# The weights of the second projection pass are loaded into another buffer, without a gate

## The chip, the cores and the metric

One Trainium2 chip, all 8 cores of it, which run the same program on different data. The metric is the device time in microseconds (us) of the slowest core.

## What is computed

One transformer layer over x of 4 x 4096 x 1024: self-attention with 16 heads, a residual and a layer norm, then a mixture of 16 experts (6 of them chosen per token), a residual and a layer norm. Cut to what matters:

```python
# L0_attn_x: (4, 4096, 1024); Wq, Wk, Wv: (1024, 1024); expert_w: (16, 1024, 1024)
q = (x @ Wq.T).reshape(N, S, H, hd).transpose(0, 2, 1, 3)
k = (x @ Wk.T).reshape(N, S, H, hd).transpose(0, 2, 1, 3)
v = (x @ Wv.T).reshape(N, S, H, hd).transpose(0, 2, 1, 3)
attn = softmax(einsum('nhqd,nhkd->nhqk', q, k) / sqrt(hd), axis=3)
x = _layernorm(x + einsum('nhql,nhld->nhqd', attn, v).transpose(0, 2, 1, 3).reshape(N, S, D))
...
for e in range(E):
    out = out + x @ expert_w[e] * gate[:, e:e + 1]
```

## The kernel before

Each core takes one of the four sequences and one half of its queries: it computes K and V for all 4096 tokens of the sequence and Q for its own 2048. There are three stages, and TensorE goes through them in program order:

1. Projections, in `proj_pass`, called for K, then V, then Q. Each pass loads one weight matrix of 1024 x 1024 (L186) and then goes through sections of 512 tokens: 8 sections for K and V, 4 for Q. A section is one load of activations (x, 1024 KB as bfloat16, L200), cast from float32 on its way, into one of two halves of a staging buffer (`xstage`). Then follow 8 groups of 8 matmuls of 128x512 (L220 for K and Q, L241 for V), each group into one of four PSUM banks, and one VectorE copy a group (L256).
2. Attention: 2 halves of the queries x 8 pairs of heads x 32 blocks of keys. TensorE computes scores (L290), ScalarE the exponentials (L350, L353), TensorE the weighted sums and the denominators (L310, L322). The operand of the scores is read from `QO`, where Q's pass put it.
3. For each of two blocks of 8 token tiles: layer norm, transposes and routing, and the 16 experts (L639), then the second layer norm.

SBUF is a few large tensors that are used again from stage to stage. `RC` (s_RC in the profile) holds during the projections the two x halves (columns 0 to 8191) and the weights `wT` (columns 8192 to 16383). `QO` (s_QO) has 16384 columns and holds Q, later the attention's output; until Q's pass writes it, nothing is in it. `RA` takes K, `RB` takes V.

The order of the loads is that of GpSimd's queue, which holds all of them: weights of K, 8 sections of x, weights of V, 8 sections of x, weights of Q, 4 sections, then 16 copies that cast the experts' weights in HBM. GpSimd issues them in this order, and one that waits holds up all that stand behind it. `tS` counts TensorE's finished groups, 8 to a section. The load of x waits until all groups but the last 8 that are queued so far are done (`ts_need = max(0, ctS.v - 8)`): section s can be loaded when section s-2 is finished, and it is the same across passes. The load of the weights waits for all groups queued so far, that is for the end of the pass before, since all three passes use `wT`:

```python
wt_gate = ctS.v
```

TensorE waits, ahead of each group, for the weights (gW0) and for its section of x (gX0 or gX1), and for the copy that frees its bank (vE).

Of the kernel before, what the change touches and what calls it, by code (L numbers as in the profile page):

```python
# [18 lines left out]
CH = 8  # L19
# [14 lines left out]
def build():  # L34
# [22 lines left out]
    v_wT = {"K": d_wkT.rearrange("(c p) j -> p c j", c=CH),  # L57
            "V": d_wvT.rearrange("(c p) j -> p c j", c=CH),
            "Q": d_wqT.rearrange("(c p) j -> p c j", c=CH)}
# [4 lines left out]
    def alloc(name, shape, dtype, psum=False):  # L64
        cm = nc.psum_tensor(name, shape, dtype) if psum else nc.sbuf_tensor(name, shape, dtype)
        t = cm.__enter__()
        cms.append(cm)
        return t
# [16 lines left out]
    QO = alloc("s_QO", [128, CH * TOK], dt.bfloat16)  # L85
# [8 lines left out]
    def bank(i, lo=0, hi=512):  # L94
        return PS[:, i * 512 + lo: i * 512 + hi]

    def xstage(par):
        return RC[:, par * 4096:(par + 1) * 4096]

    wT = RC[:, 8192:16384]  # L100
# [52 lines left out]
    cgC, ctS, ctV, csE, cvE = (Ctr() for _ in range(5))  # L153
# [7 lines left out]
    def q(eng, fn):  # L161
        SC[eng].append(fn)
# [15 lines left out]
    q("vector", f)  # L178

    def proj_pass(kind, nsect):  # L180
        wt_gate = ctS.v

        def fw(g, wsrc=v_wT[kind], wt_gate=wt_gate):
            if wt_gate > 0:
                g.wait_ge(tS, wt_gate)
            g.dma_start(out=wT.rearrange("p (c j) -> p c j", c=CH),  # L186
                        in_=wsrc).then_inc(gW[0], 16)
        q("gpsimd", fw)
        cgW[0].v += 16
        w_done = cgW[0].v  # L190
        xsrc = v_xqf if kind == "Q" else v_xfm

        for s in range(nsect):
            par = s % 2
            ts_need = max(0, ctS.v - 8)

            def fx(g, s=s, par=par, ts_need=ts_need, xsrc=xsrc):
                if ts_need > 0:
                    g.wait_ge(tS, ts_need)
                g.dma_start(out=xstage(par).rearrange("p (c t) -> p c t", c=CH),  # L200
                            in_=xsrc[:, :, s * 512:(s + 1) * 512]).then_inc(gX[par], 16)
            q("gpsimd", fx)
            cgX[par].v += 16
            x_done = cgX[par].v

            for u in range(8):
                b = ctS.v % 4
                ve_need = ctS.v - 3

                if kind in ("K", "Q"):  # L210
                    jc = u

                    def ft(t, jc=jc, b=b, par=par, x_done=x_done, w_done=w_done,
                           ve_need=ve_need):
                        t.wait_ge(gW[0], w_done)
                        t.wait_ge(gX[par], x_done)
                        if ve_need > 0:
                            t.wait_ge(vE, ve_need)
                        for dc in range(CH):
                            ins = t.matmul(  # L220
                                bank(b),
                                wT[:, dc * 1024 + jc * 128: dc * 1024 + (jc + 1) * 128],
                                xstage(par)[:, dc * 512:(dc + 1) * 512],
                                start=(dc == 0), stop=(dc == CH - 1))
                        ins.then_inc(tS, 1)
                    if kind == "K":
                        dst = RA[:, jc * SQ + s * 512: jc * SQ + (s + 1) * 512]
                    else:
                        dst = QO[:, jc * TOK + s * 512: jc * TOK + (s + 1) * 512]
                else:  # L230
                    tt, jh = u // 2, u % 2
                    kt = s * 4 + tt

                    def ft(t, tt=tt, jh=jh, b=b, par=par, x_done=x_done,
                           w_done=w_done, ve_need=ve_need):
                        t.wait_ge(gW[0], w_done)
                        t.wait_ge(gX[par], x_done)
                        if ve_need > 0:
                            t.wait_ge(vE, ve_need)
                        for dc in range(CH):  # L240
                            ins = t.matmul(  # L241
                                bank(b),
                                xstage(par)[:, dc * 512 + tt * 128:
                                            dc * 512 + (tt + 1) * 128],
                                wT[:, dc * 1024 + jh * 512: dc * 1024 + (jh + 1) * 512],
                                start=(dc == 0), stop=(dc == CH - 1))
                        ins.then_inc(tS, 1)
                    dst = RB[:, kt * D + jh * 512: kt * D + (jh + 1) * 512]

                q("tensor", ft)  # L250
                ctS.v += 1
                te_after = ctS.v

                def fv(v, dst=dst, b=b, te_after=te_after):
                    v.wait_ge(tS, te_after)
                    v.tensor_copy(dst, bank(b)).then_inc(vE, 1)  # L256
                q("vector", fv)
                cvE.v += 1

    proj_pass("K", SQ // 512)  # L260
    proj_pass("V", SQ // 512)
    proj_pass("Q", TOK // 512)
    p1_ve = cvE.v
    p1_ts = ctS.v
# [7 lines left out]
    for h in range(2):  # L272
        for c in range(NPAIR):
            p = h * NPAIR + c
# [545 lines left out]
```

## Time and profile before

| | us |
|---|---|
| median of 3 runs | 2977.89 |
| all runs | 2975.08, 2977.89, 3146.5 |
| the profiled execution, its own time | 2977.37 |
| its span on the slowest core (core 5) | 2975.8 |
| K pass, TensorE, from the first to the last matmul | 29.7 to 142.7 |
| V pass | 170.1 to 282.8 |
| Q pass | 307.4 to 364.5 |

All times inside the execution are counted from the start of the span. The span is that of the slowest core; its own time lies 1.6 us above. Attention runs to about 1636, the third stage to the end of the span.

### The profile page before, as it was taken

The page shows a single profiled execution, that of the slowest core. Times are in us where ns is not written, and L with a number is a line of the kernel's source. Part 1 is how long each engine was busy: PE and PEld are TensorE (multiplying, and loading weights), DVE is VectorE, ACT ScalarE, POOL GpSimd, SP SyncE. Part 2 cuts the span into 40 slices and gives each one's busy share as a digit, 9 for nine tenths or more (in the row PEclk, how much of TensorE's full clock was granted, in tenths as well). Part 3 has the DMA queues.
Part 4 walks back from the last instruction along what each step waited for, and adds up shares of the span by engine and source line. Part 5 has one row for each costly group of instructions (what it writes and reads, how often), then busy time and mean ns, then how long its engine had stood idle before and what let it go on. Part 6 is the DMA issues. An engine that isn't in the chain of part 4 may idle for free.

```text
span 2975.8 us, 31964 instructions; the slowest of 8 cores (2956.2 to 2975.8 us)
## 1 busy us (share of the span) xinstructions
PE 2366.3 (80%) x12032; PEld 897.2 (30%) x12032; DVE 719.1 (24%) x1555; ACT 1120.3 (38%) x1153; POOL 59.7 (2%) x80
## 2 busy tenths in 40 slices
PE   6978889888888888888888343799996343799996
PEld 2433322222222222222222111344442111344442
DVE  2323200000000000000000434233336434233336
ACT  0000089888888888888888101000000101000000
POOL 1000100000000000000000000000000000000000
PEclk9989899999999999999999666899998666899998
DMA  6464799960000000000000200221223100221221
GB/s 87 62 94 67 100 110 114 110 82 1 1 1 1 1 1 1 1 1 1 1 1 1 92 15 7 85 85 57 85 85 106 43 14 7 85 85 57 85 85 57
DMA packets 48017, 146.90 MB, mean 49 GB/s; under 512 B 2752, under 2 KB 23264, under 8 KB 46848
## 3 DMA queue, kind: packets, MB, share of 16 engines
q0 software_dynamic: 43264, 128.09, 23.4%
q1 hardware_dynamic: 4608, 16.78, 1.6%
q8 instruction: 103, 1.69, 0.2%
q14 instruction: 42, 0.34, 0.0%
HBM read 197.32 MB, written 41.94 MB: 80 GB/s over the span
## 4 chain that ended last, share of the span: by engine, by line
PE 61%; ACT 16%; DVE 9%; issue 9%; DMA 4%; DVEq 1%; ACTq 0%; POOL 0%; SPq 0%; POOLq 0%
PE s_PS L639 30%; PE s_PS L290 11%; ACT s_RC L353 9%; PE s_PS L220 6%; PE s_PS L310 5%; ACT s_RC L350 5%; PE s_PS L322 4%; PE s_PS L241 4%; DMA s_RC<-xfm 2%; DVE s_RC L462 2%; PE s_PS L377 1%; DMA s_RC<-xqf 1%; DMA s_RB<-ewb 1%; DVE s_RA L653 1%; DVE s_RC L469 1%
## 5 line engine op out<-in xcount | busy, mean ns | idle before, releaser
L639 PE MATMUL s_PS<-s_RB,s_QO 128*128 128x512 bf16 x4096 | 933.5, 391 | 138.2 <-DVE s_gates L595 67.4
L290 PE MATMUL s_PS<-s_QO,s_RA 64*128 64x512 bf16 x2048 | 598.4, 397 | 104.7 <-ACT s_RC L353 70.8
L350 ACT ACTIVATE s_RC<-s_PS,s_cb 128x1024 bf16<-128x1024 f32 x512 | 570.6, 1115 | 196.4 <-PE s_PS L290 187.3
L639 PEld LDWEIGHTS s_PS<-s_RB,s_QO 128*128 128x128 bf16 x4096 | 407.7, 100 | 660.1 <-issue 211.6
L353 ACT ACTIVATE s_RC<-s_PS,s_cb 128x1024 bf16<-128x1024 f32 x512 | 567.0, 1107 | 0.2
L310 PE MATMUL s_PS<-s_RC,s_RB 128*64 128x512 bf16 x2048 | 330.2, 401 | 10.7 <-ACT s_RC L353 10.7
L697 ACT ACTIVATE s_tE<-s_tB 128x1 f32<-128x1 f32 x16 | 3.2, 203 | 883.1 <-DVE s_tB L689 883.1
L322 PE MATMUL s_PS<-s_RC,s_ozb 128*64 128x512 bf16 x2048 | 318.0, 389 | 0.0
L367 DVE CAST s_QO<-s_PS 128x1024 bf16<-128x1024 f32 x16 | 19.6, 1225 | 1189.2 <-PE s_PS L322 1189.2
L290 PEld LDWEIGHTS s_PS<-s_QO,s_RA 64*128 64x128 bf16 x2048 | 118.1, 94 | 540.8 <-issue 540.8
L656 DVE SCALAR_TENSOR_TENSOR s_RB<-s_PS,s_gates,s_RA 128x1024 f32<-128x1024 f32 x128 | 164.2, 1283 | 275.3 <-PE s_PS L639 275.3
L220 PE MATMUL s_PS<-s_RC 128*128 128x512 bf16 x768 | 170.0, 385 | 54.3 <-DMA s_RC<-xfm 29.7
L659 DVE SCALAR_TENSOR_TENSOR s_RA<-s_PS,s_gates,s_RB 128x1024 f32<-128x1024 f32 x112 | 143.8, 1284 | 272.4 <-PE s_PS L639 272.4
L516 PE MATMUL s_PS<-s_idb,s_RC 128*128 128x128 bf16 x128 | 16.2, 305 | 190.9 <-ACT s_RC L508 190.9
L322 PEld LDWEIGHTS s_PS<-s_RC,s_ozb 128*64 128x64 bf16 x2048 | 123.1, 113 | 107.2 <-issue 10.8
L310 PEld LDWEIGHTS s_PS<-s_RC,s_RB 128*64 128x64 bf16 x2048 | 75.3, 109 | 239.8 <-issue 239.8
L350 ACT ACT_TABLE_LOAD x1 | 1.3, 1283 | 366.3 <-PE s_PS L290 366.3
L241 PE MATMUL s_PS<-s_RC 128*128 128x512 bf16 x512 | 112.7, 384 | 27.4 <-DMA s_RC<-xfm 27.4
L490 ACT ACTIVATE s_tE<-s_tB 128x1 f32<-128x1 f32 x16 | 3.2, 203 | 348.2 <-DVE s_tB L481 348.2
L220 PEld LDWEIGHTS s_PS<-s_RC 128*128 128x128 bf16 x768 | 75.9, 99 | 147.9 <-issue 60.0
L615 POOL DMA_DIRECT2D s_RB<-ewb x32 | 28.3, 885 | 2516.0 <-PE s_PS L377 1290.9
L241 PEld LDWEIGHTS s_PS<-s_RC 128*128 128x128 bf16 x512 | 50.5, 99 | 89.6 <-issue 30.6
(76 smaller groups left out, 594.2 us busy)
## 6 DMA issues: line engine op xcount, KB each, us to landing
s_RB<-ewb POOLq DMA_DIRECT2D x32, 2048.0 KB, 10.3
ewb<-ew POOLq DMA_DIRECT2D x16, 2048.0 KB, 169.3
s_RC<-xfm POOLq DMA_DIRECT2D x16, 1024.0 KB, 11.4
s_RC<-xtm SPq DMA_DIRECT2D x16, 512.0 KB, 3.6
y<-s_RC SPq DMA_DIRECT2D x16, 512.0 KB, 2.6
s_RC<-xqf POOLq DMA_DIRECT2D x4, 1024.0 KB, 17.7
s_RC<-wkT POOLq DMA_DIRECT2D x1, 2048.0 KB, 18.0
s_RC<-wvT POOLq DMA_DIRECT2D x1, 2048.0 KB, 18.2
```

Of the source, the lines that this page charges most:

```text
L220: ins = t.matmul(bank(b), wT[:, dc * 1024 + jc * 128: dc * 1024 + (jc + 1) * 128], xstage(par)[:, dc * 512:(dc + 1) * 512], start=(dc == 0 ...
L241: ins = t.matmul(bank(b), xstage(par)[:, dc * 512 + tt * 128: dc * 512 + (tt + 1) * 128], wT[:, dc * 1024 + jh * 512: dc * 1024 + (jh + 1) ...
L290: ins = t.matmul(PS[:, head * 1024 + qc * 512: head * 1024 + (qc + 1) * 512], RA[rows, c * SQ + kc * 128: c * SQ + (kc + 1) * 128], QO[row ...
L310: t.matmul(PS[orow, 2048 + qc * 512: 2048 + (qc + 1) * 512], RB[:, kcp * D + hh * 64: kcp * D + (hh + 1) * 64], P[:, head * 1024 + qc * 51 ...
L322: ins = t.matmul(PS[orow, 3072 + qc * 512: 3072 + (qc + 1) * 512], ozb[:, :], P[:, head * 1024 + qc * 512: head * 1024 + (qc + 1) * 512], ...
L350: sc.activation(P[:, 0:1024], PS[:, 0:1024], AF.Exp, bias=cb3[:, :], scale=0.125).then_inc(sE, 1)
L353: sc.activation(P[:, 1024:2048], PS[:, 1024:2048], AF.Exp, bias=cb3[:, :], scale=0.125).then_inc(sE, 1)
L377: ins = t.transpose(PS[:, 3072 + sl * 128: 3072 + (sl + 1) * 128], zs[:, sl * 128:(sl + 1) * 128], idf[:, :])
L462: v.scalar_tensor_tensor(u_f32[:, sg * 64:(sg + 1) * 64], PS[:, pcol + sg * 64: pcol + (sg + 1) * 64], rz[:, t_i * NH + sg: t_i * NH + sg ...
L639: ins = t.matmul(PS[:, pb + jh * 512: pb + (jh + 1) * 512], QO[:, dc * TOK + t_i * 128: dc * TOK + (t_i + 1) * 128], wbuf(par)[:, dc * 102 ...
L656: v.scalar_tensor_tensor(accB(tt), PS[:, pb: pb + 1024], g, accA(tt), ALU.mult, ALU.add).then_inc(vE, 1)
L659: v.scalar_tensor_tensor(accA(tt), PS[:, pb: pb + 1024], g, accB(tt), ALU.mult, ALU.add).then_inc(vE, 1)
```

## The change

V's weights go into the first 8192 columns of `QO` instead of `wT`, and their load waits for nothing. V's matmuls read them from there. The loads of K's and Q's weights are as before: K's waits for nothing, since nothing is queued ahead of it, and Q's waits for the end of V's pass. The loads of x and their waits are as before. V's and Q's x loads keep their places in the queue.

```diff
 def proj_pass(kind, nsect):
-        wt_gate = ctS.v
-
-        def fw(g, wsrc=v_wT[kind], wt_gate=wt_gate):
+        if kind == "V":
+            wtile = QO[:, 0:8192]
+            wt_gate = 0
+        else:
+            wtile = wT
+            wt_gate = ctS.v if kind == "Q" else 0
+
+        def fw(g, wsrc=v_wT[kind], wt_gate=wt_gate, wtile=wtile):
             if wt_gate > 0:
                 g.wait_ge(tS, wt_gate)
-            g.dma_start(out=wT.rearrange("p (c j) -> p c j", c=CH),
+            g.dma_start(out=wtile.rearrange("p (c j) -> p c j", c=CH),
                         in_=wsrc).then_inc(gW[0], 16)
...
-                                wT[:, dc * 1024 + jc * 128: dc * 1024 + (jc + 1) * 128],
+                                wtile[:, dc * 1024 + jc * 128: dc * 1024 + (jc + 1) * 128],
...
-                                wT[:, dc * 1024 + jh * 512: dc * 1024 + (jh + 1) * 512],
+                                wtile[:, dc * 1024 + jh * 512: dc * 1024 + (jh + 1) * 512],
```

GpSimd's queue before, from the weights of K (wkT) to the last loads of the projections (xfm is x for K and V, xqf is x for Q):

```order
L186 DMA s_RC<-wkT 128x8x1024
L200 DMA s_RC<-xfm 128x8x512 x2
L200 DMA s_RC<-xfm 128x8x512 [waits tS] x6
L186 DMA s_RC<-wvT 128x8x1024 [waits tS]
L200 DMA s_RC<-xfm 128x8x512 [waits tS] x8
L186 DMA s_RC<-wqT 128x8x1024 [waits tS]
L200 DMA s_RC<-xqf 128x8x512 [waits tS] x4
```

And now, the same stretch of the same queue:

```order
L191 DMA s_RC<-wkT 128x8x1024
L205 DMA s_RC<-xfm 128x8x512 x2
L205 DMA s_RC<-xfm 128x8x512 [waits tS] x6
L191 DMA s_QO<-wvT 128x8x1024
L205 DMA s_RC<-xfm 128x8x512 [waits tS] x8
L191 DMA s_RC<-wqT 128x8x1024 [waits tS]
L205 DMA s_RC<-xqf 128x8x512 [waits tS] x4
```

No entry has changed its place; the load of wvT has another target and has lost its wait.

TensorE's order before, at the seam from K to V (L220 is K's last group, L241 is V):

```order
L220 MATMUL s_PS<-s_RC 128x512 [waits gW0,gX1,vE]
L220 MATMUL s_PS<-s_RC 128x512 x7
L241 MATMUL s_PS<-s_RC 128x512 [waits gW0,gX0,vE]
L241 MATMUL s_PS<-s_RC 128x512 x7
L241 MATMUL s_PS<-s_RC 128x512 [waits gW0,gX0,vE]
```

And now:

```order
L225 MATMUL s_PS<-s_RC 128x512 [waits gW0,gX1,vE]
L225 MATMUL s_PS<-s_RC 128x512 x7
L246 MATMUL s_PS<-s_QO,s_RC 128x512 [waits gW0,gX0,vE]
L246 MATMUL s_PS<-s_QO,s_RC 128x512 x7
L246 MATMUL s_PS<-s_QO,s_RC 128x512 [waits gW0,gX0,vE]
```

The matmuls and their waits are the same; V's read one operand from s_QO.

## Rows read from the trace of the kernel before

**Rows 1.** The page: its head, and the chain that ended last, by engine.
```profile
span 2975.8 us, 31964 instructions; the slowest of 8 cores (2956.2 to 2975.8 us)
...
PE 61%; ACT 16%; DVE 9%; issue 9%; DMA 4%; DVEq 1%; ACTq 0%; POOL 0%; SPq 0%; POOLq 0%
```

**Rows 2.** TensorE's waits, 0 to 380 us: us in total, times, longest.
```profile
PE s_PS L220 <- DMA s_RC<-xfm: 29.7, 1, 29.7
PE s_PS L241 <- DMA s_RC<-xfm: 27.4, 1, 27.4
PE s_PS L220 <- DMA s_RC<-xqf: 24.6, 1, 24.6
```

**Rows 3.** The chain in order of time, 0 to 600 us: start, us, what.
```profile
29.72 112.93 PE s_PS L220 x512
144.04 25.77 DMA s_RC<-xfm
170.06 112.74 PE s_PS L241 x512
```

**Rows 4.** GpSimd's timeline, 100 to 150 us: start, us, instruction, idle before it.
```profile
101.74 0.87 POOL L200 DMA_DIRECT2D s_RC<-xfm  x1 [12.94 <-PE s_PS L220]
115.55 0.87 POOL L200 DMA_DIRECT2D s_RC<-xfm  x1 [12.94 <-PE s_PS L220]
143.18 0.87 POOL L186 DMA_DIRECT2D s_RC<-wvT  x1 [26.75 <-PE s_PS L220]
```

**Rows 5.** Line L200, the two loads behind the weights of K, of V, of Q.
```profile
DMA to landing us min/median/max: 24.0/27.0/30.1
...
DMA to landing us min/median/max: 25.8/27.9/30.0
...
DMA to landing us min/median/max: 23.0/25.0/27.1
```

**Rows 6.** Line L200, the load of K's last section, issued at 115.55.
```profile
DMA to landing us min/median/max: 11.3/11.3/11.3
```

**Rows 7.** Stretches around the gap ahead of V: busy us by engine, PEclk, DMA share, GB/s.
```profile
142.00:146.00 4.00, 0.64 (x3) 0.10 (x1) 0.69 (x1) 0.00 (x0) 2.62 (x3) 1.00 0.00 0
146.00:148.00 2.00, 0.00 (x0) 0.00 (x0) 0.00 (x0) 0.00 (x0) 0.00 (x0) 0.74 0.82 93
148.00:170.00 22.00, 0.00 (x0) 0.00 (x0) 0.00 (x0) 0.00 (x0) 0.00 (x0) 0.50 1.10 154
170.00:174.00 4.00, 3.94 (x10) 1.49 (x11) 0.27 (x1) 0.00 (x0) 0.00 (x0) 0.50 0.93 154
174.00:176.00 2.00, 2.00 (x11) 0.79 (x10) 0.59 (x2) 0.00 (x0) 0.00 (x0) 0.94 0.03 4
```

**Rows 8.** Line L186, the load of V's weights.
```profile
DMA to landing us min/median/max: 18.2/18.2/18.2
```

**Rows 9.** Stretches with one x load in flight, and with V's first three loads.
```profile
118.00:128.00 10.00, 10.00 (x48) 4.50 (x46) 4.15 (x6) 0.00 (x0) 0.00 (x0) 1.00 0.80 107
146.00:176.00 30.00, 5.94 (x19) 2.28 (x20) 0.86 (x2) 0.00 (x0) 0.00 (x0) 0.54 0.99 140
```

**Rows 10.** Line L200, the load of V's third section, issued at 186.63.
```profile
DMA to landing us min/median/max: 9.7/9.7/9.7
```

**Rows 11.** Groups of the page: count, busy us, mean ns of one, idle before.
```profile
L290 PE MATMUL s_PS<-s_QO,s_RA 64*128 64x512 bf16 x2048 | 598.4, 397 | 104.7 <-ACT s_RC L353 70.8
L241 PE MATMUL s_PS<-s_RC 128*128 128x512 bf16 x512 | 112.7, 384 | 27.4 <-DMA s_RC<-xfm 27.4
```

**Rows 12.** TensorE's waits on core 6, 0 to 380 us.
```profile
PE s_PS L241 <- DMA s_RC<-xfm: 24.3, 1, 24.3
```

**Rows 13.** Stretches of the third stage: the first tiles, and experts of the first block.
```profile
1636.00:1892.00 256.00, 99.83 (x469) 44.57 (x468) 102.46 (x377) 22.89 (x48) 3.58 (x4) 0.66 0.16 50
1892.00:2270.00 378.00, 374.19 (x1726) 169.03 (x1725) 148.77 (x137) 1.22 (x6) 11.48 (x13) 1.00 0.22 76
```

## The prediction

> **What bounds the kernel now.** I read the views from the outside in. The page comes first: a span of 2975.8 us, with the chain that ended last made of TensorE for 61%, ScalarE for 16% and DMA for 4% [rows 1]. That small DMA share is what the change touches, so the next view is TensorE's waits over the three projection passes. It has three long ones, and all three are for a load of activations: 29.7 us ahead of K, 27.4 us ahead of V, 24.6 us ahead of Q [rows 2]. The chain in order of time shows how the middle one is built [rows 3]: TensorE ends K at 29.72 + 112.93 = 142.65, GpSimd then issues V's weights and, behind them at 144.04, the x load of V's section 0, which lands 25.77 us later, at 169.81, and the first V matmul starts at 170.06. From 142.65 to 170.06 is 27.41 us in which VectorE and ScalarE have nothing either. Everything later in the program hangs on TensorE's order, so what this gap loses, the whole span loses.
>
> GpSimd's own rows show why [rows 4]: the loads of K run far ahead, one every 13.81 us, each issued when the section before last is done; the last (section 7) goes out at 115.55. Then the queue stands still for 26.75 us, to 143.18, because its next entry, the weights of V, waits for the end of K. The x load of V's section 0 could go when K's section 6 is done, but it stands behind that entry.
>
> **What the change does, term by term.** Chances and verdicts below use 2%, some 60 us here, as about what a measurement of this kernel can tell from no change.
>
> *The wait that goes.* The weights of V go into QO and wait for nothing, so they are issued right behind K's last x load, at 115.55 + 0.87 = 116.42 [rows 4]. The next entry, V's x section 0, waits for K's section 6. That ends one section before K: 142.65 - 13.81 = 128.84, and with the 0.53 us that lay between K's end at 142.65 and the issue at 143.18 the load is issued at 129.37. The third, V's x section 1, keeps its wait for the end of K (143.2).
>
> *What is late next.* The queue of transfers. From 115.55 on it holds K's section 7 (one unit of 1024 KB as landed), V's weights (two units), V's section 0 (one unit): four units. Three times in this trace the same four units went out in one piece: weights, x, x. The second x load landed 30.1 us after its issue ahead of K, 30.0 ahead of V and 27.1 ahead of Q [rows 5]; the two issues before it take 0.9 us each, so the four units needed 31.9, 31.8 and 28.9 us from the first issue. So V's section 0 lands between 115.55 + 28.9 = 144.4 and 115.55 + 31.9 = 147.4 if the four units run without a break. The other end adds the pieces one behind the other: K's section 7 alone took 11.3 us [rows 6], to 126.9; the weights first showed traffic some 3 us after their issue (no DMA at all in 142 to 146 [rows 7]) and took 18.2 us [rows 8], so 15.2 us behind another transfer, to 142.1; the x load landed 8.4 us after the weights (169.8 against 143.2 + 18.2 = 161.4), to 150.5. A check by DMA busy share: one x load alone was 10 us x 0.80 = 8.0, the four units ahead of V 30 us x 0.99 = 29.7, 7.4 a unit [rows 9]. Section 7 and three such units make 30.2; at the share of 1.10 seen in full flow [rows 7] that is 27.5 us of traffic, which begins some 3 us after the first issue: it ends at 146, and the last completion comes behind it. I take a landing at 148.6 and, with 0.25 us from landing to first matmul (169.81 to 170.06), a start of V at 148.8. It leans to the later half because the x loads of K take 11.3 us even alone, against 9.7 for the first one that goes out alone in V's pass [rows 10]. The gap shrinks from 27.4 to 6.2 us, and V starts 170.06 - 148.8 = 21.3 us sooner.
>
> *Is K's last section held up?* Its data must be there at 128.84; alone it landed at 126.9, and it is ahead of the weights in the queue. The slack is 2 us. If the weights' packets mixed with it, it could be late by some 4 us (its 8 us of traffic stretched to 12), but V's own data would not come earlier or later by that: the same bytes pass before V can start. A stall there only splits the gap in two. I cost it at nothing for the sum.
>
> *The clock.* After K the granted clock is still 1.00 to 146, falls within 146 to 148 (mean 0.74), and stays at 0.50, the 1.2 GHz level, through the gap and to 174; over the next 2 us its mean is 0.94, so it is back at 1.00, 2.4 GHz, just after 174 [rows 7]. TensorE so works for about 4.2 us at half clock, which costs 2.1 us: the V pass took 112.7 us [rows 3], 110.6 of them by full clock. With a start at 148.8 the clock has fallen as well, and the same 2.1 us are paid (1.5 to 3 by where the rise comes). Only if V starts before 147.0 is this term saved. I take 0, with up to 2.1 us as the favourable end.
>
> *Reading the weights from QO.* 512 matmuls of V take their moving operand from another tensor. The nearest row that streams from s_QO is the score matmul, 397 ns against 384 ns for V's [rows 11]. The upper end is 13 ns x 512 = 6.7 us; but those matmuls stand among clock changes and use half the rows, and a busy time of pipelined matmuls is not their spacing, so I take 0. Below nothing has no reason. Nothing else uses QO before Q's pass writes it, and Q's copies come after V's last matmul in VectorE's order.
>
> *What stays.* Q's weights wait for the end of V as before, so the 24.6 us ahead of Q remain. The load of V's section 1 is issued at 143.2, lands behind section 0 at 155 or so, and is needed after 148.8 + 15 = 164: hidden by the eight groups of section 0. The expert casts are issued after Q's loads, and all shift together.
>
> **The sum.** The profiled execution took 2977.4 us around its span of 2975.8: 2977.4 - 21.3 = 2956.1. That execution stands 0.5 us under the median of 2977.9, so the forecast for the median is 2956 us. By the ends above the likely case alone runs from 2977.4 - 25.4 - 2.1 = 2950 to 2977.4 - 19.3 + 6.7 = 2965.
>
> The Trainium skill ("DMA: Bandwidth & Descriptors", section "Anatomy of one DMA") gives a fit for such a load: 2.0 us plus its bytes at 436 GB/s. By it the weights (4 MB as read) would take an estimated 11.6 us; the trace has 18.2 [rows 8], so the fit is too fast here, and the sum goes by the rows.
>
> **The rivals.**
>
> *A. The transfers queue up worse: 2964 us.* Each load pays its full time alone, one behind the other: 126.9 + 18.2 + 11.3 = 156.4, V starts at 156.6, 13.4 us are won. For it: the x loads of K take 11.3 us though nothing else is in flight. Against it: the three runs of four units all took 28.9 to 31.9 us [rows 5]. Chance 0.12.
>
> *B. The gap closes: 2948 us.* Both loads land before 142.65 and the clock never falls: 27.4 + 2.1 = 29.5 us won. For it: on core 6 the gap was 24.3 us, by its own waits [rows 12], and a load of V's pass takes 9.7 us. Against it: even the fastest of the three runs of four units ends at 144.4. A start between 144.4 and 147.0 lies between, at 2950 to 2952. Chance of the closed gap 0.10. By the fit of the Trainium skill cited above the estimated landing would lie before K's end, so it speaks for this rival; the 18.2 us of the row speak against it.
>
> *C. Slower: V's pass runs at a lower clock, 3011 us.* The 27 us rest between two dense passes goes. If the granted clock then sank over V's pass to the 0.66 that it has over the stretch of the first tiles after attention [rows 13], the 110.6 us of matmuls at full clock would take 167.6, 54.9 more than now, and 54.9 - 21.3 = 33.6 are lost. It decides from a mean clock of 110.6 / (112.7 + 21.3) = 0.83 in V's pass; below that the change loses. Against it: TensorE ran 378 us in the expert stage at a mean of 1.00 [rows 13] with hardly a rest. The Trainium skill ("TensorE: Matmul & The Clock Gate", note on the peak-current limiter) says that dense matmuls on three or more cores of a die bring the clock to 13/16; no row here shows such a level in K's or V's pass, and those are already dense on all eight cores. Chance 0.02.
>
> *D. The gain is given back: 2977 us.* Attention, or the stretch of the first tiles, could lose by its place what V wins. For it: the cores differ by up to 20 us in the whole span [rows 1], so stages are not rigid. Against it: no instruction waits for a clock time or another core, and the loads there start after Q. Chance 0.02.
>
> **How the numbers follow.** Likely case 0.74, A 0.12, B 0.10, C 0.02, D 0.02. To hold 8 in 10 the range reaches from rival B less the spread of two runs of 3 us (2945) to rival A with the same (2967). Faster by over 2% would need 60 us, more than twice the gap: 0.01. Slower by over 2% is only a much harsher C: 0.01. Within 2%: 0.98.
>
> **What would show it.** In the changed kernel GpSimd issues V's weights at about 116.4 and x at 129.4; TensorE's wait ahead of V is about 6 us, still for the x load; K's pass stays at 112.9 us; V's pass stays at 112 to 114 us with the clock low for its first 3 to 5 us; the wait ahead of Q is still 24 to 25 us; attention and the experts last as long as before. I am wrong if the wait ahead of V is above 15 us or below 3, if a wait appears inside K's pass that moves V, or if later stages lose more than 5 us.

## The result, and the profile after

| | before | after |
|---|---|---|
| the profiled execution, us | 2977.37 | 2954.78 |
| its span on the slowest core | 2975.8 (core 5) | 2953.3 (core 7) |
| ratio after to before, 95% interval | | 0.9925 (0.9912 to 0.9939) |
| predicted | | 2956 (2945 to 2967) |

The ratio makes 2955.4 us of the median of before in the same comparison, 2977.77 us: 22 us less, clear of noise and well inside 2%. Some executions of every program in this study, the unchanged one too, had a lower clock on one die or both and took longer; they are left out of all comparisons.

The head and the chain of the page after, beside [rows 1]:

```profile
span 2953.3 us, 31963 instructions; the slowest of 8 cores (2933.4 to 2953.3 us)
...
PE 62%; ACT 15%; DVE 9%; issue 9%; DMA 3%; DVEq 1%; ACTq 0%; POOL 0%; SPq 0%; POOLq 0%
```

DMA has gone from 4% to 3% of the chain: one of the three long waits is what left it. TensorE's waits from 0 to 380 us, beside [rows 2] (us in total, times, longest):

```profile
PE s_PS L225 <- DMA s_RC<-xfm: 30.9, 2, 28.6
PE s_PS L225 <- DMA s_RC<-xqf: 25.4, 1, 25.4
PE s_PS L246 <- DMA s_RC<-xfm: 2.9, 1, 2.9
```

L225 and L246 are L220 and L241 of before. The wait ahead of V fell from 27.4 to 2.9 us, the one ahead of Q stayed. But the first row has two waits now: 28.6 us ahead of K and, new, 30.9 - 28.6 = 2.3 us inside K. The chain in order of time shows where, beside [rows 3]:

```profile
28.62 99.66 PE s_PS L225 x448
128.81 18.39 DMA s_RC<-xfm
147.44 112.11 PE s_PS L246 x512
260.94 23.72 DMA s_RC<-xqf
284.90 58.08 PE s_PS L225 x256
```

K's 448 matmuls up to the end of section 6 run until 128.28. What the end hangs on then is the load issued at 128.81, not the last section of K. V starts at 147.44 instead of 170.06. GpSimd's timeline from 90 to 300 us, beside [rows 4]:

```profile
114.99 0.88 POOL L205 DMA_DIRECT2D s_RC<-xfm  x1 [12.94 <-PE s_PS L225]
115.86 0.88 POOL L191 DMA_DIRECT2D s_QO<-wvT  x1
128.81 0.87 POOL L205 DMA_DIRECT2D s_RC<-xfm  x1 [12.06 <-PE s_PS L225]
145.11 0.87 POOL L205 DMA_DIRECT2D s_RC<-xfm  x1 [15.43 <-PE s_PS L225]
```

The weights of V leave with no idle time ahead of them, and the x load of V's section 0 leaves when K's section 6 is done. The landings of the first two of these loads, line L205 and then line L191, beside [rows 6] and [rows 8]:

```profile
DMA to landing us min/median/max: 15.4/15.4/15.4
...
DMA to landing us min/median/max: 26.3/26.3/26.3
```

The last x load of K was 11.3 us on its way when it was alone and takes 15.4 with the weights behind it, and the weights take 26.3 in place of 18.2. The clock around the seam, beside [rows 7] (busy us by engine, then PEclk, DMA share, GB/s):

```profile
128.00:130.00 2.00, 0.26 (x2) 0.00 (x0) 0.69 (x1) 0.00 (x0) 0.87 (x1) 1.00 1.01 131
130.00:132.00 2.00, 1.41 (x7) 0.71 (x8) 0.00 (x0) 0.00 (x0) 0.00 (x0) 1.00 1.05 167
...
146.00:148.00 2.00, 0.56 (x2) 0.28 (x3) 0.00 (x0) 0.00 (x0) 0.00 (x0) 0.74 0.13 13
148.00:150.00 2.00, 2.00 (x7) 0.63 (x5) 0.00 (x0) 0.00 (x0) 0.00 (x0) 0.50 1.02 145
150.00:152.00 2.00, 2.00 (x10) 0.88 (x9) 0.69 (x1) 0.00 (x0) 0.00 (x0) 0.91 1.18 174
```

At 128 to 131 TensorE stands with the DMA engines full: this is the new stall. At 146 to 150 the granted clock still falls to its half, but it is back just after 150, 3 us after V's start.

The two profiled executions are told by their slowest cores, 5 before and 7 after. Over all eight cores the mean span fell by 24.2 us, from 2968.5 to 2944.3.

Behind Q nothing moved: from the end of Q to the end of the span were 2975.8 - 364.5 = 2611.3 us before, and are 2953.3 - (284.90 + 58.08) = 2610.3 now.

### The profile page after: what moved, and what is told of

Its sections match the earlier page's. It is cut to its first block, busy times and chain, and to the rows that moved or that the text cites. A ratio compares the mean times of both kernels' runs of the same rounds, so it can differ in the third digit from the quotient of the medians.

```text
span 2953.3 us, 31963 instructions; the slowest of 8 cores (2933.4 to 2953.3 us)
## 1 busy us (share of the span) xinstructions
PE 2366.6 (80%) x12032; PEld 896.9 (30%) x12032; DVE 719.0 (24%) x1555; ACT 1121.0 (38%) x1153; POOL 59.8 (2%) x80
## 4 chain that ended last, share of the span: by engine, by line
PE 62%; ACT 15%; DVE 9%; issue 9%; DMA 3%; DVEq 1%; ACTq 0%; POOL 0%; SPq 0%; POOLq 0%
PE s_PS L644 30%; PE s_PS L295 11%; ACT s_RC L358 9%; PE s_PS L315 5%; PE s_PS L225 5%; ACT s_RC L355 4%; PE s_PS L327 4%; PE s_PS L246 4%; DVE s_RC L467 2%; DMA s_RC<-xfm 1%; DMA s_RC<-xqf 1%; PE s_PS L382 1%; DMA s_RB<-ewb 1%; DVE s_RA L658 1%; DVE s_RC L474 1%
## 5 line engine op out<-in xcount | busy, mean ns | idle before, releaser
L225 PE MATMUL s_PS<-s_RC 128*128 128x512 bf16 x768 | 171.7, 387 | 56.3 <-DMA s_RC<-xfm 30.9
L225 PEld LDWEIGHTS s_PS<-s_RC 128*128 128x128 bf16 x768 | 76.2, 100 | 151.3 <-issue 64.5
L246 PE MATMUL s_PS<-s_QO,s_RC 128*128 128x512 bf16 x512 | 112.1, 382 | 2.9 <-DMA s_RC<-xfm 2.9
L521 PEld LDWEIGHTS s_PS<-s_idb,s_RC 128*128 128x128 bf16 x128 | 12.4, 139 | 198.4 <-issue 198.4
## 6 DMA issues: line engine op xcount, KB each, us to landing
s_RC<-xfm POOLq DMA_DIRECT2D x16, 1024.0 KB, 11.6
s_QO<-wvT POOLq DMA_DIRECT2D x1, 2048.0 KB, 26.3
```

What stands on the lines that cost most here:

```text
L225: ins = t.matmul(bank(b), wtile[:, dc * 1024 + jc * 128: dc * 1024 + (jc + 1) * 128], xstage(par)[:, dc * 512:(dc + 1) * 512], start=(dc = ...
L246: ins = t.matmul(bank(b), xstage(par)[:, dc * 512 + tt * 128: dc * 512 + (tt + 1) * 128], wtile[:, dc * 1024 + jh * 512: dc * 1024 + (jh + ...
```

## The experiments

All are edits of the changed kernel, and each time is compared with the kernel before on the same chip. All compute what the reference does; one of them loads a matrix a second time, to a place that nothing reads. Where waits are compared, they are those of the slowest core of the profiled execution.

### Is it the wait, or the place of the operand?

```diff
         if kind == "V":
             wtile = QO[:, 0:8192]
-            wt_gate = 0
+            wt_gate = ctS.v
```

> V's weights go into QO as in the change, but their load keeps the wait for the end of K. Theory (the whole gain is the wait that went; where V's operand is read from costs nothing): the wait ahead of V is back at 24 to 27 us, V's pass at 112 to 113 us, time 2977 us, ratio to before 1.000 within 0.001. Rival (the place of the operand has a price or a gain of its own, up to 13 ns on each of 512 matmuls): 2971 or 2984 us, and V's pass 6 us shorter or longer.

Measured: ratio 0.9996 (0.9983 to 1.0009). TensorE's wait ahead of V and, from the page, the group of V's matmuls:

```profile
PE s_PS L246 <- DMA s_RC<-xfm: 27.2, 1, 27.2
```
```profile
L246 PE MATMUL s_PS<-s_QO,s_RC 128*128 128x512 bf16 x512 | 113.2, 385 | 27.2 <-DMA s_RC<-xfm 27.2
```

The group answers to that of L241 in [rows 11]: 385 ns against 384, with the operand in another tensor. The place has no cost that these runs can show, to within 0.13% (4 us), and the wait is the whole gain.

### What decides when V starts?

First, the weights are issued one section later, so that K's last x load is alone:

```diff
         if kind == "V":
             wtile = QO[:, 0:8192]
-            wt_gate = 0
+            wt_gate = ctS.v - 8
```

> V's weights go into QO, but their load waits until K's section 6 is done, so it is issued at about 128.8 and the x load at 129.7, and K's last x load is alone in flight. Theory (V starts when the bytes queued since the first issue have passed): weights and x need 26.6 us as in the kernel before, so V starts at about 155.5, the stall of 2.3 us inside K is gone, the wait ahead of V is about 13 us, time 2964 us. Rival (the 2.3 us stall inside K is itself paid in the total): V starts as early as now or earlier, at 145 to 147, time 2953 us.

Measured: 2963.75 and 2963.82 us. Its TensorE waits on the slowest core:

```profile
PE s_PS L225 <- DMA s_RC<-xfm: 30.1, 1, 30.1
PE s_PS L225 <- DMA s_RC<-xqf: 25.4, 1, 25.4
PE s_PS L246 <- DMA s_RC<-xfm: 12.2, 1, 12.2
```

and its chain in order of time:

```profile
130.43 24.37 DMA s_RC<-xfm
155.03 113.41 PE s_PS L246 x512
```

The first row is back at one wait: the stall inside K is gone once the weights are not behind K's last load, which landed in 11.2 us here. And yet the kernel is 9 us slower than with the change: the weights are issued at 129.56 in place of 115.86, 13.7 us later, x only 1.6 us later (130.43 against 128.81), and V starts 7.6 us later and spends 1.3 us more in its own pass. This edit moves two things at once, the stall and the issue of the weights. That the stall of 2.3 us was no cost of the change follows from the chain of the page after: V's start hung on the x load issued at 128.81, not on the section that was held up, and the stall lay beside the transfers that V waited for anyway.

Second, the bytes are raised. V's weights are loaded a second time, into the unused half of QO, and V waits for both:

```diff
         q("gpsimd", fw)
         cgW[0].v += 16
+        if kind == "V":
+            def fw2(g, wsrc=v_wT[kind]):
+                g.dma_start(out=QO[:, 8192:16384].rearrange("p (c j) -> p c j", c=CH),
+                            in_=wsrc).then_inc(gW[0], 16)
+            q("gpsimd", fw2)
+            cgW[0].v += 16
```

> As the change, but V's weights are loaded twice, the second time into the other half of QO, where nothing reads them; V waits for both. Computation is unchanged. Theory (the queued bytes set V's start): two more units at 7.4 us, V starts some 14.8 us later, at about 162, wait ahead of V 17 to 19 us, time 2970 us. Rival (a latency or the issue at 128.8 sets it, not the bytes): V starts within 3 us of the change's 147.4, time 2956 us.

Measured: 2966.4 us in one run. TensorE's wait ahead of V, and then the chain in order of time:

```profile
PE s_PS L252 <- DMA s_RC<-xfm: 17.2, 1, 17.2
```
```profile
128.34 32.55 DMA s_RC<-xfm
161.13 112.95 PE s_PS L252 x512
```

The x load leaves at the same time as with the change, 128.3, and lands 32.6 us later instead of 18.4, because two more units are in the queue: 14.2 us, where 14.8 were expected. So V's start goes with the bytes in flight; a latency of the x load, or the moment of its issue alone, would have left it where it was. The total came out 3.6 us better than expected, of which the trace shows 1 us in V's start; one run doesn't settle the rest.

Third, the same bytes earlier. The weights are queued behind the x load of K's section 6:

```diff
-        q("gpsimd", fw)
-        cgW[0].v += 16
+        if kind != "V":
+            q("gpsimd", fw)
+            cgW[0].v += 16
...
             q("gpsimd", fx)
+            if kind == "K" and s == nsect - 2:
+                def fwv(g):
+                    g.dma_start(out=QO[:, 0:8192].rearrange("p (c j) -> p c j", c=CH),
+                                in_=v_wT["V"]).then_inc(gW[0], 16)
+                q("gpsimd", fwv)
+                cgW[0].v += 16
```

> As the change, but V's weights are queued behind the x load of K's section 6 instead of section 7, one section of 13.8 us earlier. Theory (bytes): the queue is drained before K ends, the wait ahead of V is 0 to 1 us, a stall of 2 to 5 us moves to the head of K's section 6 or 7, the clock does not fall and V's pass takes 110.6 us instead of 112.1; V starts at 145 to 147, time about 2952 us. Rival (a stall inside K costs nothing, as the prediction had it): V starts at 142.7 plus nothing, time 2948 us.

Measured: 2952.9 and 2955.5 us, ratio 0.9925 (0.9896 to 0.9953), no better than the change. First TensorE's waits in K, then the chain in order of time, then the page's group of V's matmuls:

```profile
PE s_PS L232 <- DMA s_RC<-xfm: 33.3, 2, 29.5
```
```profile
100.68 16.79 DMA s_RC<-xfm
117.72 15.65 PE s_PS L232 x64
133.51 13.97 PE s_PS L232 x64
147.49 110.52 PE s_PS L253 x512
```
```profile
L253 PE MATMUL s_PS<-s_QO,s_RC 128*128 128x512 bf16 x512 | 110.7, 379 | 0.0
```

V no longer waits at all, and starts at 147.5 all the same. The stall of 33.3 - 29.5 = 3.8 us now stands ahead of section 6, whose 64 matmuls take 15.65 us instead of 13.97: the granted clock has dropped there, to 0.50 from 118 to 121. Now that V starts when K ends, the stall is paid in full. The rival, that a stall inside K is free, fails here; it held in the change, where V waited for its loads anyway.

### What is left to win

The weights of V in four pieces, each of 512 KB as landed, behind the x loads of K's sections 3 to 6:

```diff
-        q("gpsimd", fw)
-        cgW[0].v += 16
+        if kind != "V":
+            q("gpsimd", fw)
+            cgW[0].v += 16
...
             q("gpsimd", fx)
+            if kind == "K" and 3 <= s <= 6:
+                def fwv(g, i=2 * (s - 3)):
+                    g.dma_start(out=QO[:, i * 1024:(i + 2) * 1024].rearrange(
+                                    "p (c j) -> p c j", c=2),
+                                in_=v_wT["V"][:, i:i + 2, :]).then_inc(gW[0], 16)
+                q("gpsimd", fwv)
+                cgW[0].v += 16
```

> V's weights go into QO in four pieces of a quarter, queued behind the x loads of K's sections 3 to 6. Theory (bytes spread out fit into the pauses of the queue, 8 + 3.7 us of traffic in each 13.8): V's data are there when K ends, the wait ahead of V is 0 to 0.5 us, the clock does not fall, V's pass takes 110.7 us; V starts at 143 plus whatever stalls inside K remain (0 to 3 us in all), time 2948 to 2951 us, ratio 0.990 to 0.991. Rival (each piece delays the x load ahead of it by its whole 3.7 us, more than the slack of 2): four stalls of about 1.7 us, V starts at 149 to 150, time 2955 us as with the change.

Measured: ratio 0.9904 (0.9856 to 0.9953); six of the seven times that enter it lie from 2949.1 to 2954.1 us, the seventh is 2974.0. On the slowest core, TensorE's waits in K and then the chain in order of time:

```profile
PE s_PS L233 <- DMA s_RC<-xfm: 32.2, 3, 30.2
```
```profile
89.50 55.41 PE s_PS L233 x256
144.91 110.52 PE s_PS L254 x512
```

Two stalls of 2.0 us together are left, K's later sections run through, and V follows K without a gap, at 144.9. V's pass takes 110.5 us in place of 112.1 at a clock that stays up, so it ends at 255.4 against 259.6. Against the change this is 4 us in the trace; by the times alone the two intervals overlap, so this gain is not shown.

Then Q's weights in the same way, behind the x loads of V's sections 3 to 6, into wT, which K's weights have left (the lines with a minus are those of the run before):

```diff
-        if kind != "V":
+        if kind == "K":
...
-            if kind == "K" and 3 <= s <= 6:
+            if kind != "Q" and 3 <= s <= 6:
+                nt = QO if kind == "K" else wT
+                nw = v_wT["V" if kind == "K" else "Q"]
...
+                    if gate > 0:
+                        g.wait_ge(tS, gate)
```

where the gate is 64, the end of K, for Q's pieces.

> As the pieces for V, and Q's weights likewise in four pieces behind the x loads of V's sections 3 to 6, into the buffer that K's weights have left (they wait for the end of K, not of V). Theory (the gap ahead of Q is the same case as that ahead of V): the wait of 24 to 25 us ahead of Q goes too, and its 2 us of low clock, Q starts at 254 to 256, time 2921 to 2925 us, ratio 0.981 to 0.983. Rival (the later stages give it back, or the pauses in V's pass don't hold the pieces): ratio 0.985 or above.

Measured: ratio 0.9818 (0.9790 to 0.9847), 2922.3 to 2926.6 us. The chain of its slowest core:

```profile
119.09 27.79 PE s_PS L238 x128
146.88 55.27 PE s_PS L259 x256
203.18 12.90 DMA s_RC<-xfm
216.32 41.60 PE s_PS L259 x192
257.92 55.27 PE s_PS L238 x256
```

Q starts at 257.9 with no wait ahead of it; with the change it was 284.9. The stalls inside K are larger on this core (33.0 - 29.2 = 3.8 us in four waits), so it is 2 us behind the range expected; the other cores start Q at 252 to 255.

Last, the start of K, with its weights in two halves by columns and the first x load between them (again against the run before):

```diff
-            q("gpsimd", fw)
+            def fh(g):
+                g.dma_start(out=wT.rearrange("p (c j) -> p c j", c=CH)[:, :, 0:512],
+                            in_=v_wT["K"][:, :, 0:512]).then_inc(gW[0], 16)
+            q("gpsimd", fh)
...
+            if kind == "K" and s == 0:
+                def fh2(g):
+                    g.dma_start(out=wT.rearrange("p (c j) -> p c j", c=CH)[:, :, 512:1024],
+                                in_=v_wT["K"][:, :, 512:1024]).then_inc(gW[1], 16)
+                q("gpsimd", fh2)
+                cgW[1].v += 16
...
+                           ve_need=ve_need, half=(kind == "K" and jc >= 4)):
                         t.wait_ge(gW[0], w_done)
+                        if half:
+                            t.wait_ge(gW[1], 16)
```

> As the pieces for V and Q, and K's weights are loaded in two halves by columns, with the first x load between them, so that K's first group needs two units instead of three. Theory (bytes queued set the start of a pass, here too): K starts one unit, 6.5 to 7.5 us, sooner, at about 22.5; section 0 does not wait for the second half; time 2914 to 2918 us, ratio 0.979 to 0.981. Rival (the second half comes too late, or the halves are slower by their shorter rows): K starts at 22 to 25 but stalls at its fifth group by 3 us or more, and less than 4 us is won.

Measured: ratio 0.9796 (0.9768 to 0.9825), 2917.2 to 2920.1 us, the fastest version of this study by its times (the intervals of this ratio and the last overlap). The same kernel was run once more, and its trace is the one read:

> The run with K's weights in halves once more, on the same chip: K starts at 25 to 27 us, time 2917 to 2920 us, ratio 0.979 to 0.981.

Measured: 2916.4 and 2916.9 us. TensorE's waits in K on its slowest core, and then GpSimd's timeline of the first loads:

```profile
PE s_PS L249 <- DMA s_RC<-xfm: 27.2, 2, 25.7
```
```profile
4.75 0.92 POOL L195 DMA_DIRECT2D s_RC<-wkT  x1
5.62 0.92 POOL L209 DMA_DIRECT2D s_RC<-xfm  x1
6.49 0.93 POOL L214 DMA_DIRECT2D s_RC<-wkT  x1
7.36 0.93 POOL L209 DMA_DIRECT2D s_RC<-xfm  x1
```

K starts at 25.7, not at 22.5: two units in place of three now have to land first, yet it wins only 3.5 us on the slowest core (25.7 against 29.2 in the run before), not 7. The other cores start K at 23.9 to 25.5, where it was 28.6 to 30.9. The suspicion is the same as at K's last load, that the loads queued behind take their share. So the second half is held back until the first x load has landed:

```diff
                 def fh2(g):
+                    g.wait_ge(gX[0], 16)
                     g.dma_start(
```

> As the run with K's weights in halves, but GpSimd issues the second half (and the second x load behind it) only when the first x load has landed. Theory (loads that are queued together share the engines, so the later ones delay the earlier): with two units alone in flight K starts at 22 to 23 us instead of 25 to 27; the second half, issued at about 22, lands near 33 and stalls K's fifth group by 0 to 2 us, the second x load lands near 41 and may stall section 1 by 1 to 3 us; time within 3 us of the run with halves (2917 to 2920). Rival (the loads go strictly one behind the other, and two units simply take 20 us at the start): K starts at 25 to 27 as there, and the delayed second half costs 5 us or more of stalls.

Measured: 2918.9 us in one run. TensorE's waits on the slowest core:

```profile
PE s_PS L250 <- DMA s_RC<-xfm: 22.8, 1, 22.8
...
PE s_PS L250 <- DMA s_RC<-wkT: 3.2, 1, 3.2
```

K starts at 22.8, 2.9 us sooner, and on all eight cores between 22.2 and 23.3, where it was 23.9 to 25.7. What is won is lost again at the fifth group, which waits 3.2 us for the second half; this stall is above the 2 us expected, and the time is no better than with the halves alone. The first x load landed 17.0 us after its issue here and 20.0 us with two more loads behind it. So loads in flight together slow each other, though they are issued one after the other; how they share the DMA engines was not looked at.

## Why the prediction was right

*The wait that goes*: as forecast. Issues at 115.86 and 128.81, where 116.42 and 129.37 were worked out; K had begun 1.1 us sooner on this core.

*What is late next*: the right term, a little too large. The x load landed at 147.20; the run of four units as one piece gave 144.4 to 147.4, the pieces end to end 150.5, and I had chosen 148.6. From the first issue at 114.99 it is 32.2 us, next to the 31.8 and 31.9 us of [rows 5] (the third stretch there had 28.9). Of the 1.4 us between 148.6 and 147.2, 0.6 is that earlier first issue and 0.8 the term itself. The estimate from the same four units in another order was the better one; the pull towards the sum of separate times was not needed. V's start came 22.6 us sooner instead of 21.3, and the profiled execution became 22.6 us shorter. That these two agree to a tenth is in part luck, since they compare different cores, and K began 1.1 us sooner on the later one. The runs with the later issue and with doubled weights agree with a term that is set by bytes in flight.

*Is K's last section held up?* The text left it open and named some 4 us; the load landed 4.1 us later than alone. That this is free for the sum held: V's start hung on the x load issued at 128.81, and the run that avoids the stall is 9 us slower. What I did not follow through is how it shows: K's pass is 144.56 - 28.62 = 115.9 us long where "stays at 112.9" was written, and the wait ahead of V is 2.9 us where about 6 was. Of the 3.3 us between, 1.9 are K's later end (144.56 against 142.65: the stall of 2.3 and 0.7 in K's matmuls, less the 1.1 by which K started earlier) and 1.4 the earlier landing. With "below 3" I had named a wait of this size as a sign against me; that bound forgot that a stall inside K shortens the wait behind it.

*The clock*: right for the slowest core, where the clock falls to 0.50 and V's pass takes 112.1 us. On cores 1 and 2 the wait ahead of V is 1.7 and 1.9 us and their V passes take 110.7 us; the runs without a gap have 110.7 us as well. So the price of the low clock at a restart is 1.3 to 2.9 us here (V's passes of 111.97 us on core 5 of this run to 113.41 with the later issue, against 110.5 to 110.7); the forecast was 2.1, within 1.5 to 3. What did not hold is "only if V starts before 147.0 is this term saved". It came from a clock that fell 4.3 us after K's end; on the slowest core it now fell 2.4 us after K's end (144.56 to 147.0), and cores 4, 5 and 6 started V before 147.0 and paid all the same. Core 4, its V pass with the wait ahead of it, and then a stretch of its clock:

```profile
142.67 112.35 PE L246 MATMUL s_PS<-s_QO,s_RC 128*128 128x512 bf16 x512 [2.32 <-DMA s_RC<-xfm]
```
```profile
144.00:146.00 2.00, 2.00 (x6) 0.73 (x5) 0.66 (x1) 0.00 (x0) 0.00 (x0) 0.50 1.19 181
```

Its clock was still at 1.00 when V began and fell at about 143.7. The equally long stall inside K on core 7, 128.28 to 130.6, left the clock at 1.00. So the length of the gap alone does not say here whether the price is paid, and what does is not shown.

*Reading the weights from QO*: no cost shows, by the run that changes only this.

*The rivals.* A (the loads pay their full time alone, V at 156.6) fell: 147.4. B (no gap) fell by 3 us, and the 18.2 us of the weights became 26.3 rather than the 11.6 that the fit of the Trainium skill gives; the trace disagrees with that fit still more than before, here with other loads in flight. C fell: over V's pass the granted clock has a mean of 0.99. D fell: the stages behind Q take 1 us less than before.

The limiter that the Trainium skill describes ("TensorE: Matmul & The Clock Gate", note on the peak-current limiter) shows in none of the traces compared here, though in the run with V's and Q's pieces the three passes follow each other on all eight cores with hardly a rest and V's takes 110.8 us. A level like it does show in another trace of this study, the first of the kernel with K's weights in halves: on cores 0 and 1 the granted clock had a mean of 0.81 over V's pass, which took 134.6 us, while cores 2 to 6 had 1.00 and took 110.7 us. From core 1:

```profile
154.97 134.61 PE L270 MATMUL s_PS<-s_QO,s_RC 128*128 128x512 bf16 x512
```

So rival C named a kind of loss that these passes can have; nothing here shows that the change brings it.

## What to carry to other kernels

A wait at the head of a queue of loads costs what stands behind it too: here one gate on a weights buffer also held back an x load that now leaves 15 us earlier (128.8 against 144.0). Once the gate is gone, the next bound is the number of bytes issued since the queue was last empty, and a stretch of the trace in which the same bytes went out in one piece gives an estimate of the landing: two of the three such stretches here were within half a microsecond of the 32.2 us measured, the third was 3.3 us short. A big prefetch can be cut into pieces that fit into the pauses of the stream it shares, since in one piece it delayed even the load ahead of it; with both V's and Q's weights in pieces the kernel gained 1.8% (ratio 0.9818), where the change alone gained 0.75%. A stall of that kind was free while the next stage waited for its data anyway, and was paid once it didn't.

## What had not been expected

A load is delayed by one issued behind it on the same queue: 11.3 us alone, 15.4 with the weights issued 0.87 us later. At the start of K, two loads of one unit each let TensorE begin at 22.8 us when alone and at 25.7 with two more behind them. And the clock after short gaps: waits of 1.7 and 1.9 us ahead of V left it at 1.00 on two cores, waits of 2.3 to 3.6 us on the other six all met a drop to about 0.50, yet a stall of 2.3 us inside K left it at 1.00.
